# Second layer of a two-layer graph network: 64 groups of nodes per window in place of 32

## What is computed

```
h = relu(layernorm(x))
c = concat(h[src], h[dst], rel[type]) @ W1 + b1          # per edge
alpha = softmax over the edges of one node of leaky_relu(c @ w2)
x = x + leaky_relu(segment_sum(c * alpha, dst))          # first layer
h = relu(layernorm(x))
agg = segment_sum(h[src], dst)
x = x + where(a node has an edge, agg, h)                # second layer
```

## Time and profile before

| | |
|---|---|
| median of 3 runs | 1560.09 us (1557.64 to 1561.22) |
| profiled execution | 1562.62 us |
| its span, first to last instruction | 1558.3 us |
| busy share PE, DVE, ACT, POOL | 85%, 87%, 85%, 69% |
| POOL's first gather of the second layer starts at | 999.71 us |
| its last one starts at | 1533.47 us |

### The profile page before, as it was taken

One profiled execution on the slowest core, in us unless ns is written; L12 is line 12 of the kernel. 1 busy time (PEld: TensorE's weight loads), 2 busy tenths in 40 slices (PEclk: granted clock), 3 DMA queues, 4 the chain that ended last, 5 costly groups with the idle time before them and its releaser, 6 DMA issues.

```text
span 1558.3 us, 34077 instructions
## 1 busy us (share of the span) xinstructions
PE 1317.2 (85%) x11994; PEld 1280.0 (82%) x11995; DVE 1356.0 (87%) x3631; ACT 1328.2 (85%) x3500; POOL 1072.4 (69%) x969
## 2 busy tenths in 40 slices
PE   1598999999999999999999999358776777777776
PEld 0488999999999999999999999357666777767666
DVE  6678999999999999999999988848888787877876
ACT  0697999899989999999999997279899898998987
POOL 5678887767667788786766720277777777777772
PEclk9999999999999999999999999878999989999998
DMA  4865867777777777788677855639898888889875
GB/s 112 243 183 151 201 207 210 208 220 192 209 194 217 210 190 217 208 223 214 193 208 209 219 163 155 178 107 253 236 251 241 248 236 246 249 240 253 245 199 153
DMA packets 466205, 322.96 MB, mean 207 GB/s; under 512 B 31028, under 2 KB 433030, under 8 KB 466034
## 3 DMA queue, kind: packets, MB, share of 16 engines
q1 hardware_dynamic: 434274, 257.30, 59.9%
q0 software_dynamic: 31760, 63.49, 14.8%
HBM read 216.17 MB, written 104.45 MB: 206 GB/s over the span
## 4 chain that ended last, share of the span: by engine, by line
PE 49%; POOL 24%; DVE 9%; issue 9%; ACT 3%; DMA 3%; POOLq 0%; SPq 0%; ACTq 0%; DVEq 0%
POOL xe L1168 17%; PE c_p L1674 7%; PE c_p L1675 6%; POOL xn L1168 6%; PE c_p L1677 5%; PE t_p L1662 4%; PE t_p L1660 3%; PE t_p L1656 3%; PE y_p L1692 3%; PE y_p L1691 3%; PE y_p L1693 3%; PE y_p L1690 3%; PE t_p L1659 3%; PE c_p L1721 2%; POOL xe L1160 2%
## 5 line engine op out<-in xcount | busy, mean ns | idle before, releaser
L1160 POOL DMA_INDIRECT xe<-in_x,idx_t x516 | 637.8, 1236 | 224.6 <-issue 134.3
L1168 POOL DMA_INDIRECT xe<-x_d,idx x320 | 313.9, 981 | 129.2 <-issue 96.0
L1577 ACT ACTIVATE an<-xn,nbias,rstd 128x128 f32<-128x128 f32 x783 | 326.8, 482 | 4.0 <-DVE nbias L1298 4.0
L1267 DVE BATCH_NORM_STATS2 st<-xe 128x6 f32<-128x256 f32 x434 | 171.0, 413 | 66.5 <-DMA xe<-x_d,idx 66.2
L1580 ACT ACTIVATE ae<-xe,nbias,rstd 128x128 f32<-128x128 f32 x522 | 226.3, 482 | 0.0
L1674 PE MATMUL c_p<-w1a,th 128*128 128x129 f32 x1044 | 215.4, 288 | 0.0
L1267 DVE BATCH_NORM_STATS2 st<-xn 128x6 f32<-128x256 f32 x440 | 169.7, 413 | 42.5 <-DMA xn<-x_d,idx 20.8
L1675 PE MATMUL c_p<-w1b,th 128*128 128x129 f32 x1044 | 202.3, 276 | 0.0
L1384 DVE TENSOR_SCALAR sel<-row,plc_t,alpha 128x256 f32<-128x256 bf16 x522 | 190.4, 404 | 3.4
L1677 PE MATMUL c_p<-relk,ot 128*128 128x129 bf16 x1566 | 176.5, 221 | 0.0
L1721 PE MATMUL c_p<-cs,ot 128*128 128x128 f32 x792 | 118.0, 319 | 65.2 <-ACT cs L1602 63.4
(11 more groups left out here) (210 smaller groups left out, 3556.9 us busy)
## 6 DMA issues: line engine op xcount, KB each, us to landing
xn<-in_x SPq DMA_DIRECT2D x130, 384.0 KB, 7.4
x_d<-xn SPq DMA_DIRECT2D x130, 384.0 KB, 8.0
xn<-x_d SPq DMA_DIRECT2D x194, 256.0 KB, 4.6
out<-xn SPq DMA_DIRECT2D x194, 256.0 KB, 3.2
plr<-place_d SPq DMA_DIRECT2D x65, 464.0 KB, 4.2
tyr<-types_d SPq DMA_DIRECT2D x65, 256.0 KB, 6.1
xe<-in_x,idx_t POOLq DMA_INDIRECT x522, 6.7
xe<-x_d,idx POOLq DMA_INDIRECT x320
```

What stands on the lines that cost most here:

```text
L1160: nc.gpsimd.indirect_dma_start(out=xe_of(u)[:, e, :], out_offset=None, in_=x, in_offset=bass.IndirectOffsetOnAxis(ap=idx_t[:, j:j + 1], ax ...
L1168: nc.gpsimd.indirect_dma_start(out=xe2_of(u)[:, e, :], out_offset=None, in_=x1_d, in_offset=bass.IndirectOffsetOnAxis(ap=idx2[:, j:j + 1], ...
L1267: return v.bn_stats(st[:, j % 2, c:c + 2, :].rearrange("p c t -> p (c t)"), rows_.rearrange("p r d -> p d r"))
L1577: a(an[:, u % 2, i, :], xs_of(u)[:, i, :], ACT.Relu, bias=nbias1[:, c:c + 1], scale=rstd1[:, c:c + 1])
```

## The change

A window becomes eight units (64 groups, `PW = 8`), so that there are 13 windows in place of 25. A full window has 33 tiles, each two groups after the one before, and each tile serves four groups (the first and the last two). Whole windows of before had 17 tiles per 32 groups. The last window has 14 groups and eight tiles in both.

The tables are made in four rounds of nine tiles each. The partitions are now slots of 13 windows one after the other (9 x 13 = 117), without gaps, so that a slot's instructions can't start at a multiple of 32; in place of pieces, all 117 partitions hold all values and a 0/1 matrix `of_slot` picks those of the round by a product and a sum. POOL writes two tables of numbers for it (`bases2`, at unit 90), DVE makes the 0/1 matrix and the numbers to subtract at steps 102 to 105 (`T_PICK`), and picks the starts in the two steps behind the chain. The chain and the test have 33 links in place of 17. The rounds begin at step 172 in place of 150; the last one ends at the same step, 245. SP writes the last border's copies with one DMA in place of 18, and reads the borders back with 18 in place of eight. In `select2` the 0/1 matrix of every fourth unit is in two buffers.

```diff
-PW = 4
+PW = 8
-SPANS = ((0, 2), (1, 3), (3, 3), (5, 3), (6, 4), (8, 4), (10, 4), (12, 4), (14, 4), (16, 4), (18, 4), (20, 4), (22, 4),
-         (24, 4), (26, 4), (28, 4), (30, 2))
+SPANS = tuple((max(2 * k - 2, 0), min(2 * k + 2, UGW) - max(2 * k - 2, 0)) for k in range(UGW // 2 + 1))
-R2 = 32
-ROUNDS = -(-PT // 4)
+SLOTS2 = 9
+ROUNDS = -(-PT // SLOTS2)
-T_COUNT, T_CHAIN, T_WINDOW, T_APART = 60, 110, 150, 22
+T_COUNT, T_BASE, T_PICK, T_CHAIN, T_WINDOW, T_APART = 60, 90, 102, 110, 172, 22
...
-                    for at in range(0, 4 * R2, R2):
+                    for at in range(0, rows2, NW):
...
-                        for n in range(UN * NU, NW * UGW + 1):
-                            sp.dma_start(borders_d[n:n + 1, :], borders[TU - 1:TU, TC - 1, UN - 1:UN]).then_inc(k_moved2, 16)
+                        sp.dma_start(borders_d[UN * NU:NW * UGW + 1, :].unsqueeze(0),
+                                     borders[TU - 1:TU, TC - 1, UN - 1:UN].unsqueeze(1).to_broadcast([1, NW * UGW + 1 - UN * NU, 1])).then_inc(k_moved2, 16)
...
+                def bases2():
+                    pool.wait_ge(k_borders, 1)
+                    g = nc.gpsimd
+                    g.iota(window_of, pattern=[[rows2, ROUNDS], [-NW, PT]], base=0, channel_multiplier=1, allow_small_or_imprecise_dtypes=True)
+                    g.memset(starts2[:, 0:1], -2.0 * P)
+                    g.iota(starts2[:, 1:PT], pattern=[[-2 * P, PT - 1]], base=-2 * P, channel_multiplier=0, allow_small_or_imprecise_dtypes=True
+                           ).then_inc(k_row2, 1)
...
+                    if s == T_PICK:
+                        dve.wait_ge(k_row2, 1)
+                        b.mark(v.tensor_scalar(of_slot, window_of, 0.0, None, ALU.is_ge))
+                    if s == T_PICK + 1:
+                        b.settle()
+                        b.mark(v.scalar_tensor_tensor(of_slot, window_of, float(NW), of_slot, ALU.is_lt, ALU.mult))
+                        b.mark(v.scalar_tensor_tensor(chosen, window_of, -float(UGW * P), starts2.unsqueeze(1).to_broadcast([rows2, ROUNDS, PT]),
+                                                      ALU.mult, ALU.add))
+                    if s == T_PICK + 2:
+                        b.settle()
+                        b.mark(v.tensor_tensor(chosen, chosen, of_slot, ALU.mult))
+                    if s == T_PICK + 3:
+                        b.settle()
+                        b.mark(v.tensor_reduce(minus2, chosen, AX, ALU.add))
...
-                    if 0 <= k < ROUNDS:
-                        for h, rows_ in enumerate(quarters):
-                            t = min(4 * k + h, PT - 1)
-                            v.tensor_scalar(minus2[rows_, k:k + 1], col[rows_, 0:1], -float(UGW * P),
-                                            float(UGW * P * rows_.start - SPANS[t][0] * P - 2 * P), ALU.mult, ALU.add)
...
                     if k == PT:
                         b.settle()
-                        for h, rows_ in enumerate(quarters):
-                            last = v.tensor_copy(at2[rows_, 0:len(range(h, PT, 4))], from2[rows_, h:PT:4])
-                        last.then_inc(k_borders, 1)
+                        b.mark(v.tensor_tensor(chosen, of_slot, from2[:, 0:PT].unsqueeze(1).to_broadcast([rows2, ROUNDS, PT]), ALU.mult))
...
+                        if i == 1:
+                            b.mark(v.tensor_reduce(first2, chosen, AX, ALU.add))
+                        if i == 2:
+                            v.tensor_copy(at2, first2).then_inc(k_borders, 1)
```

More of the change, by code:

```diff
@@ L555, in gnn_two_layers @@
         plc2 = sb("plc2", [P, PT * NW], f32)
-        small2 = sb("small2", [P, 94], f32)
+        small2 = sb("small2", [P, 15 + UGW + 1 + 2 * (PT + 1) + 2 * ROUNDS], f32)
         borders = small2[0:TU, 0:9].rearrange("p (k i) -> p k i", i=UN)
         counts = small2[0:TU, 9:15].rearrange("p (k i) -> p k i", i=2)
[L559 to L562, removed]
+        rows2 = SLOTS2 * NW
+        columns2 = list(itertools.accumulate((15, UGW + 1, PT + 1, PT + 1, ROUNDS, ROUNDS)))
+        ends2, from2, wrong2, minus2, at2 = (small2[0:rows2, lo:hi] for lo, hi in itertools.pairwise(columns2))
+        at2 = at2.bitcast(i32)
         spare1 = sb("spare1", [P, 3 * P], f32)
@@ L1195, in gnn_two_layers, with sel2_of @@
             spare = cs[:, :, :, :].rearrange("p a b c -> p (a b c)")
[L1196 to L1198 removed]
+            WIDE = max(sum(n for k, g, n, c in spans2(u)) for u in range(PW)) * P
+            RING = 5
+            EDGES = RING * UT * D
+            edge2 = spare[:, 0:EDGES].rearrange("p (u e d) -> p u e d", u=RING, d=D)
             SEL2 = 4
+            FIT = 4 * UE * PLACES // P * P
             spare_sel = [selT[:, :, :, :].rearrange("p u e s -> p (u e s)"), ot[:, :, :, :].rearrange("p q i s -> p (q i s)").bitcast(f32),
[L1202 to L1206 removed]
+                         sel[:, :, :, :].rearrange("p u e s -> p (u e s)"), spare[:, EDGES:EDGES + WIDE]]
+            rest_sel = spare[:, EDGES + WIDE:EDGES + WIDE + WIDE - FIT]
+            assert EDGES + WIDE + WIDE - FIT <= CR * UE * (D + 2) and WIDE <= 8 * SLOTS
+            def sel2_of(u, at, n):
+                if u % SEL2 == 0 and at >= FIT:
+                    return rest_sel[:, at - FIT:at - FIT + n]
+                return spare_sel[u % SEL2][:, at:at + n]
             sums2 = [y_p, c_p, t_p, sb_p]
@@ L1391, in select2 @@
                     wait(dve, L2.y, u - SEL2 + 1)
-                    at, to = 0, sel2_of(u)
+                    at = 0
                     for k, first, n, c in spans2(u):
                         j, n = NW * k + u // PW, n * P
-                        last = v.tensor_scalar(to[:, at:at + n], row2[:, c * P:c * P + n], plc2[:, j:j + 1], ones[:, 0:1], ALU.is_equal, ALU.mult)
+                        last = v.tensor_scalar(sel2_of(u, at, n), row2[:, c * P:c * P + n], plc2[:, j:j + 1], ones[:, 0:1], ALU.is_equal, ALU.mult)
                         at += n
@@ L1461, in second_tables @@
                         return
[L1462 to L1463 removed]
+                    n = NW * min(SLOTS2, PT - SLOTS2 * k)
+                    filled = slice(rows2 * k, rows2 * k + n)
                     b = borders_steps
@@ L1601, in norm2 @@
                         c = (UT + 1) * at + (e if e < UT - 1 else UT)
-                        last = a(edge2[:, u % (PW + 1), e, :], xe2_of(u)[:, e, :], ACT.Relu, bias=nbias2[:, j % 2, c:c + 1], scale=rstd2[:, j % 2, c:c + 1])
+                        last = a(edge2[:, u % RING, e, :], xe2_of(u)[:, e, :], ACT.Relu, bias=nbias2[:, j % 2, c:c + 1], scale=rstd2[:, j % 2, c:c + 1])
                     last.then_inc(L2.nrm, 1)
```

40 lines of the change are left out of this document (20 added, 20 removed).

## The result

| | time (us) | against the kernel before |
|---|---|---|
| changed kernel | 1538.20, median of 4 runs (1537.80 to 1539.34) | 1558.87 beside it, 4 runs (1557.47 to 1561.22); ratio 0.9867, 95% interval 0.9855 to 0.9879 |
| the same, measured again | 1539.47, 4 runs (1537.52 to 1540.13) | 1558.65, 23 runs; ratio 0.9872, interval 0.9854 to 0.9889 |
| profiled execution | 1539.34, span 1535.5 | 1562.62, span 1558.3 |

One more run also moved the base: 1558.87 in place of 1560.09.

What follows compares the result with a forecast made beforehand. PE was taken to bound the first layer, POOL's gathers the second. -15.0 + 0.4 + 0.4 - 2.05 = -16.25 us from the profiled 1562.62 gave 1546.4, or 1543.8 us on the median's scale; range 1540 to 1552.

Steps and rivals of the forecast that it cites:

- Rivals 1 to 6: DVE/ACT bound second layer 0.09; matrices lock POOL 0.05; DVE bounds first layer 0.05; DMA 0.04; PE slower 0.03; general path 0.01.
- -2.05: First layer, summed: 2.15 us gained, 0.3 lost to new instructions, 0.2 gained by a round of tables; between -2.7 and +4.8.
- -15.0 + 0.4 = -14.6: Second layer's gathers: twelve fewer save 15.0 us, wider 0/1 matrices on DVE cost 0.4 us.
- +0.4: End of second layer: PE's extra products in the last unit but one lose 0.4 us, between 0 and 0.7.
- 2.15 us gained: First layer: PE's idle time at 440 to 480 us goes with DVE's 20 small instructions of L1427; 2.15 us or nothing.
- Its two windows with idle time: First layer: PE's windows at 440 to 480 us, busy 18.91 and 18.94 of 20, 2.15 us lost.
- the 0.3 us forecast for all that is new: First layer: added DVE instructions and links of chain and test cost 0.3 us; bounds 0 and 6.9.
- 0.2 for the round: First layer: one round of tables fewer, two PE transposes of 264 ns, gains 0.2 us, between 0 and 0.5.
- rival 3: DVE bounds the first layer too, which gives +4.8 us in place of -2.05: 1550.7 us; chance 0.05.
- the late part of the steps: Second layer: 0.028 us per gather step beyond the bare 1.252, 11.6 us over 413 steps, put down to DVE's matrices.
- I take 0.4: Second layer: 7.0 us more of DVE matrices delay POOL's gathers by 0.4 us; bounds 0 to 7.0.
- I take 15.0: Second layer: twelve gathers fewer on POOL at the bare step of 1.252 us save 15.0 us.

Runs made afterwards that it cites:

- a: Kernel before, with its 20 small instructions of L1427 spread one per step over steps 80 to 99: 1557.88 us, ratio 0.9995.
- b: Kernel before, with the same 20 small instructions ordered by quarter of the partitions, five per step: 1558.69 us, ratio 0.9987.
- the five named under f: Executions with 404 gathers and all matrices: changed kernel twice, and with 20 small instructions added in three placements; first to last gather 515.1 to 516.4 us.
- f: Changed kernel with twelve gathers put back, one per full window, into a scratch tile: 1554.67 us, ratio 0.9965.
- h: Changed kernel with 75 more 0/1 matrices of 512 columns written into a scratch tile: 1546.84 us, ratio 0.9920.
- g: Changed kernel writing only the last of a unit's five 0/1 matrices from the fifth unit on, so its sums are wrong: 1530.47 us, one run.
- c: Changed kernel with 20 small instructions put back, four per step on the four partition quarters, into unread columns: 1542.97 us, ratio 0.9900.
- d: Changed kernel with 20 small instructions put back, four per step, all on partitions 0 to 31: 1539.34 us, ratio 0.9866.

## Why the prediction missed

**Mechanism.** It was right in the main. PE bounds the first layer and POOL the second; twelve gathers went, and the windows of the 20 small instructions filled. Rivals 1 to 6 didn't come: POOL waits 0.3 us for a unit's sum, ACT at 93.37 still waits, DMA engines stand at 0.84, the clock at 0.95.

**The sizes,** column by column of the table of rulers, each as the mean of the executions with either code in that part (before: the two of before, a and b, in the first layer the two of before alone; changed: the five named under f, in the first layer the two of changed):

| part | forecast | measured |
|---|---|---|
| 41st to last copy | -2.05 | 761.6 - 765.3 = -3.7 |
| first to last gather | -15.0 + 0.4 = -14.6 | 515.8 - 532.4 = -16.6 |
| last gather to end | +0.4 | 25.5 - 25.1 = +0.4 |
| sum | -16.25 | -19.9 |

The timed differences are 20.7 and 19.2 us. That the last row comes out as forecast is partly luck: that column scatters by 0.5 us with the same code.

*First layer: the failed step is "2.15 us gained".* It took the idle time from PE's busy column, and of two windows alone. "Its two windows with idle time" is a misreading: the same trace lost time at 500 to 520 us, where the casts of L1436 lie, and the sum has no term for them. By the copies the pieces cost 3.0 us in place of 2.15, and the casts' stretch 0.7 to 0.8 in place of nothing. Other columns of the same rows were nearer: PEld has 18.04 and 18.44 in the two windows, 3.0 us less than the changed kernel's 19.81 and 19.71; 186 + 183 matmuls where a full window has 202 are 35 missing, at 10.1 per us 3.5 us. Also the step priced the 20 pieces by their length alone, 2.8 us, and took them as one kind with the new links. But three of four were held, with the instruction behind them, and the links (all on partitions from 0) overlap. What is new costs 0.1 to 0.3 us up to the 111th copy, where the picks lie; from the 141st copy to the last both kernels need 415.0 to 415.2 us, the test's links among it and a round of tables gone. So the 0.3 us forecast for all that is new, less 0.2 for the round, held, and rival 3 did not come true.

*Second layer: the failed step is that the late part of the steps stays and grows ("I take 0.4" for the matrices, and behind "I take 15.0" that the rest of a step "isn't removed").* The bare price held: f's twelve gathers take 15.1 us of their own. But what the steps last beyond 1.250 us sums up to 10.2 to 12.5 us in the four executions with the old code and to 8.9 to 10.0 in the five with the new one: on average it fell by 1.6 us. These 1.6 and the 15.0 make the 16.6 measured. The wider matrices brought no lateness that shows: f, which has them and 416 gathers, lies at 10.9, among the old ones. By the fraction measured in h their 7.0 us would be 0.6, an estimate, and such scatter hides that. Why the late part fell isn't settled; the difference is less than the scatter of the old code, and the trace that the forecast stood on had the most of all, 12.5.

*Base.* The median that the forecast stood on came from three runs, 1560.09; beside the result it was 1558.87, on the three later occasions 1558.65, 1560.13 and 1559.96. Of the 5.6 us between 1543.8 and 1538.20, 3.65 are the two terms, 1.2 the base, and the remaining 0.7 lies within the scatter of the columns that the change doesn't touch. The range failed because both terms fell outside their bounds: it allowed 2.7 us for the first layer and 15.4 for the second, and 3.7 and 16.2 were measured (16.6 less the 0.4 at the end).

None of these kernels beats the changed one with the whole computation done. Run g bounds what there is left to gain from the matrices: some 9 us, if they could be kept off the gathers. That wasn't tried.

## What to carry to other kernels

Where PE is the bound, don't read a stall from its busy time alone: look at the weight loads' column and the count of matmuls against a full window, in every window, and measure between two instructions that repeat once per unit. Price an instruction on a loaded DVE by its distance from its neighbours, and keep small ones on the partitions that the neighbours start from; if pieces must lie elsewhere, order them so that the first partition changes seldom. Where one queue is the bound and its work is removed, price it by the bare step, keep the late part as a term of its own with the scatter of several traces as its bounds, and put the removed work back in a run of its own to learn the price.

## What the runs showed of the hardware

- A DVE instruction that starts on other partitions than the one before lost the overlap: it started 0.01 to 0.03 us after its end, in place of about 0.07 before it. Four small ones took 0.62 us up to the start of the product behind them, in place of 0.25 (c against d). Twenty of them cost the first layer 3.0 us and 0.6.
- DVE's 0/1 matrices lengthened gathers on POOL beside them: 42.4 us more of them, 5.0 us more of the stage (3.5 from the third gather on); four of five left out, 200 us, 8.7 us less.
- A gather of 128 rows took POOL 0.94 us, and 1.249 to 1.252 us passed from start to start in the median (g's mean step, with most matrices left out, 1.252).
- The first 41 units took 193.4 to 197.0 us from one execution to the next, with the same code; from there to the last copy, executions with equal code in that part lie within 0.6 us of each other.
